# Attention on one core: reciprocals of the softmax sums taken on 16 columns after a trip through DMA, and weighting steps issued in four pairs a group

## The chip, the cores and the metric

The kernel runs on one core of a Trainium2 chip. The metric is the time of one execution on the device in microseconds, given as the median of several runs. The profile is of one further execution, with its own time. TensorE is called PE here, VectorE DVE, ScalarE ACT, GpSimd POOL, and SyncE, which issues most of the transfers, SP.

## The reference

Four gated residual blocks follow each other on x (2 batches, 512 tokens, width 1024): a quantised product with the context, a feed-forward layer with eight low-rank adapters, a cross-attention on the context, and a mixture of 2 experts out of 3. The change lies in the third block. Cut to it:

```python
q = (query @ Wq).reshape(b, sq, 32, 32).transpose(0, 2, 1, 3)   # 32 heads of 32
k = (key @ Wk).reshape(b, sk, 8, 32)...                         # 8 key/value heads
v = (value @ Wv).reshape(b, sk, 8, 32)...
k = jnp.repeat(k, 4, axis=1); v = jnp.repeat(v, 4, axis=1)
scores = jnp.einsum('bhqd,bhkd->bhqk', q, k) * 32 ** (-0.5)
probs = jax.nn.softmax(scores, axis=-1)                         # over 1024 keys
out = jnp.einsum('bhqk,bhkd->bhqd', probs, v)
x = x + jnp.tanh(g_xattn[1]) * (out @ Wo)
```

## The kernel before

The whole program is written out engine by engine, and semaphores alone order the engines. The attention is cut into 16 groups (2 batches by 8 key/value heads). A group has 4 query heads, 512 queries and 1024 keys, and 32 steps. In step `t` of group `g` PE issues, in this order:

- a *row score tile* (L866, `score_step`): queries on the partitions, 512 keys across, for a group further on (52 steps ahead). It goes to one of three PSUM banks (`s_bank`). DVE takes the maximum of each row from it (L1609, `maximum`), and frees the bank by that. The 32 pairs of maxima of a group are folded by one small reduction (L1616, `mxc`).
- a *turned score tile* (L948, in `group`): keys on the partitions, 512 queries across, with the row maximum subtracted by two extra rows of the operands. It goes to one of three other banks (`T_BANKS`). ACT takes the exponential from it (L1265) into `PB`, and frees the bank by that. Eight tiles of 128 keys by four heads make the 32 steps.
- in some steps, behind these, *weighting steps* (L879, `weigh`): the exponentials of 128 keys, four heads, times the values, in f32, 8 instructions each, into bank 5. Eight a group.
- in steps 2 and 18 one of the two `total` steps (L879 as well, with `onesf` as weights, 8 instructions): the sums of the exponentials of the group before, into bank 6, on all 32 partitions of a head alike.

In this text a *burst* is what PE issues of L879 in one go, and a *run* the steps between two bursts. Before the change a weighting step follows steps 2, 6, 10, ... 30, so that a group has six bursts with one L879 step and two bursts (at 2 and 18) with two, and runs of four steps.

Once a group, at `TURN_AT`, PE turns the folded maxima of the next group (L874), ACT copies them (L1240, `row_out`), DVE makes their remainder (L1624, `row_lows`, at `ROW_LO_AT`), and SP sends both rows into the query operand. The turned maxima take one of the three banks of the turned tiles, from `TURN_AT` until `row_lows` has read them; the turned tile of step `TURN_AT + 3` is the next to use that bank and waits for `row_lo`.

The rest of a group's work: POOL adds the exponentials in pairs of key tiles (L590, four a group) and sends the sums on by an accumulating transfer; ACT copies the weighted values out at step 3 (L1246), the sums at step 20 (L1256, into `p_total`) and the divided output at step 28 (L1250). DVE takes the reciprocals of the sums of the group before the last in four quarters of 128 columns (L1599, `invert`), at steps 2, 6, 10 and 14. POOL multiplies by them behind its second addition of a group (L572, `divide`), and makes the remainder behind its third (L577).

SP goes through each group in this order: the two maxima rows of the group (L428), then, once the last turned tile of the group before is done, the queries (L421) and keys (L415) of the group two ahead, three transfers each.

Groups 14 and 15 have few or no row score tiles left; in their place PE issues parts of the output projection (L911).

## Time and profile before

| | us |
|---|---|
| median of 3 runs | 1292.96 (1292.89 to 1294.55) |
| the profiled execution, its time | 1290.26 |
| its span, first to last instruction | 1288.4 |

Busy shares of the span: PE 97%, DVE 63%, POOL 53%, ACT 38%. The attention loop lies between 458 and 865 us. A PE instruction that waits for nothing starts about 0.22 us after the one before it; the duration that the profile gives for it (0.38 us) includes its way through the array, so successive ones overlap and the starts are what counts. The same holds for DVE and ACT in a smaller measure: the start of the next says how long an instruction holds its engine.

### The profile page before, as it was taken

The page shows a single profiled execution, that of the slowest core. Times are in us where ns is not written, and L with a number is a line of the kernel's source. Part 1 is how long each engine was busy: PE and PEld are TensorE (multiplying, and loading weights), DVE is VectorE, ACT ScalarE, POOL GpSimd, SP SyncE. Part 2 cuts the span into 40 slices and gives each one's busy share as a digit, 9 for nine tenths or more (in the row PEclk, how much of TensorE's full clock was granted, in tenths as well). Part 3 has the DMA queues.
Part 4 walks back from the last instruction along what each step waited for, and adds up shares of the span by engine and source line. Part 5 has one row for each costly group of instructions (what it writes and reads, how often), then busy time and mean ns, then how long its engine had stood idle before and what let it go on. Part 6 is the DMA issues. An engine that isn't in the chain of part 4 may idle for free.

```text
span 1288.4 us, 17618 instructions
## 1 busy us (share of the span) xinstructions
PE 1243.5 (97%) x6696; PEld 532.5 (41%) x6696; DVE 814.6 (63%) x1433; ACT 487.7 (38%) x853; POOL 680.7 (53%) x300
## 2 busy tenths in 40 slices
PE   7879989999999989999999999999999999999998
PEld 4545544444444422222222222234554444444444
DVE  6677762233345678989998999625555855737632
ACT  3459431011110157777777777762163010010000
POOL 6000997720004268889889888991073553534510
PEclk8989999999999999999999999999999999999999
DMA  8347133200024224545444544431063342533301
GB/s 327 115 137 255 33 115 115 83 16 0 1 64 131 90 66 110 111 90 119 109 106 97 115 109 101 90 75 33 17 214 114 98 148 88 176 112 98 114 6 60
DMA packets 44524, 130.69 MB, mean 101 GB/s; under 512 B 6817, under 2 KB 17057, under 8 KB 40353
## 3 DMA queue, kind: packets, MB, share of 16 engines
q1 hardware_dynamic: 37536, 91.94, 22.1%
q0 software_dynamic: 4608, 33.56, 12.9%
q10 hardware_dynamic: 2304, 4.20, 0.9%
q8 instruction: 47, 0.77, 0.2%
q14 instruction: 29, 0.23, 0.1%
HBM read 85.49 MB, written 10.49 MB: 74 GB/s over the span
## 4 chain that ended last, share of the span: by engine, by line
PE 76%; DVE 16%; ACT 3%; issue 3%; DMA 1%; SPq 1%; POOL 1%; ACTq 0%; POOLq 0%; DVEq 0%
PE bank L624 45%; PE bank L879 9%; DVE mxp L1609 7%; PE bank L911 7%; PE bank L866 6%; PE bank L948 5%; DVE xn L1599 2%; PE bank L699 1%; DVE R L1349 1%; PE bank L711 1%; ACT XTh L1088 1%; DVE stats L1362 1%; DMA b1t<-b_in 1%; DVE XTl L1496 1%; ACT R L1086 1%
## 5 line engine op out<-in xcount | busy, mean ns | idle before, releaser
L1609 DVE TENSOR_REDUCE mxp<-bank 128x1 f32<-128x512 f32 x512 | 320.3, 680 | 59.2 <-PE bank L866 58.9
L1265 ACT ACTIVATE R<-bank 128x512 f32<-128x512 f32 x512 | 273.8, 601 | 114.6 <-PE bank L948 111.6
L624 PE MATMUL bank<-XTh,R 128*128 128x512 bf16 x896 | 277.7, 379 | 0.0
L590 POOL TENSOR_TENSOR R<-R 128x2048 f32<-128x2048 f32 x48 | 218.7, 4558 | 35.5 <-ACT R L1265 29.5
L624 PE MATMUL bank<-R 128*128 128x512 bf16 x960 | 209.2, 379 | 0.0
L624 PE MATMUL bank<-XTl,R 128*128 128x512 bf16 x448 | 169.9, 379 | 0.0
L612 POOL TENSOR_TENSOR R<-stage_pair,R 128x1024 bf16<-128x1024 f32 x32 | 75.0, 2359 | 144.8 <-DVE R L1758 86.5
L624 PEld LDWEIGHTS bank<-R 128*128 128x128 bf16 (+1 forms) x960 | 93.9, 98 | 113.3
L866 PE MATMUL bank<-R 96*128 96x512 bf16 x352 | 134.6, 382 | 4.8 <-DVE mxp L1609 3.0
L879 PE MATMUL bank<-R,stage_c 128*32 128x512 f32 x1024 | 136.4, 604 | 0.5 <-ACT R L1265 0.5
L948 PE MATMUL bank<-R 98*128 98x512 bf16 x352 | 133.9, 380 | 1.9 <-ACT R L1265 1.9
L624 PEld LDWEIGHTS bank<-XTh,R 128*128 128x128 bf16 x896 | 87.8, 98 | 105.1 <-issue 0.6
L500 POOL TENSOR_TENSOR R<-stage_pair,zero 128x1024 f32 (+1 forms) x35 | 67.4, 1926 | 88.8 <-DMA stage_pair<-wts_in 75.7
L612 POOL TENSOR_TENSOR R<-stage_c,R 128x1024 bf16<-128x1024 f32 x32 | 73.6, 2312 | 53.6 <-DVE R L1758 50.2
L1323 ACT ACTIVATE R<-bank,b1t 128x512 f32<-128x512 f32 x32 | 21.9, 687 | 206.4 <-PE bank L624 206.4
L1496 DVE TENSOR_TENSOR XTl<-bank,XTh 128x512 bf16<-128x512 f32 (+1 forms) x48 | 30.7, 681 | 82.2 <-ACT XTh L1181 80.0
L866 PEld LDWEIGHTS bank<-R 96*128 96x128 bf16 x352 | 34.1, 97 | 112.8 <-DVE mxp L1609 85.5
L502 POOL TENSOR_TENSOR R<-stage_pair,R 128x1024 f32 (+1 forms) x35 | 75.4, 2153 | 5.3 <-POOL R L500 4.7
L1599 DVE RECIPROCAL xn<-p_total 128x128 f32<-128x128 f32 x64 | 59.2, 937 | 27.7 <-POOL xn L572 27.7
L590 POOL TENSOR_TENSOR stage_pair<-R 128x2048 f32<-128x2048 f32 x16 | 73.9, 4616 | 2.3 <-ACT R L1265 1.2
L532 POOL TENSOR_TENSOR X<-X,R 128x1024 f32<-128x1024 f32 x8 | 18.6, 2349 | 101.7 <-DVE R L1489 101.7
L649 PE MATMUL bank<-R 128*128 128x512 bf16 x192 | 51.5, 424 | 20.4 <-DVE R L1349 13.7
(194 smaller groups left out, 1598.5 us busy)
## 6 DMA issues: line engine op xcount, KB each, us to landing
stage_pair<-wts_in SPq DMA_DIRECT2D x35, 512.0 KB, 3.6
R<-R POOLq DMA_DIRECT2D x16, 1024.0 KB, 7.0
stage_pair<-R POOLq DMA_DIRECT2D x16, 1024.0 KB, 7.0
stage_pair<-w_in SPq DMA_DIRECT2D x32, 512.0 KB, 3.5
stage_c<-w_in SPq DMA_DIRECT2D x32, 512.0 KB, 3.6
R<-q_scr SPq DMA_DIRECT2D x48, 128.0 KB, 2.4
XTh<-ctx_nat_in SPq DMA_DIRECT2D x11, 512.0 KB, 4.0
XTh<-ctx_t_in SPq DMA_DIRECT2D x9, 512.0 KB, 5.1
```

The source lines that it names most:

```text
L500: pool.tensor_tensor(hi, stage_w[stage][:, :], zero[:, :].to_broadcast([P, D]), ALU.add).then_inc(wt_hi, 1)
L502: pool.tensor_tensor(lo, stage_w[stage][:, :], hi, ALU.subtract).then_inc(wt_done, 1)
L590: pool.tensor_tensor(PS[(0, 1, 2, 1)[j]], PB[2 * j % 4], PB[2 * j % 4 + 1], ALU.add).then_inc(p_add, 1)
L612: pool.tensor_tensor(lo[:, cols], stage_e[(n - N_WT) % RING_E][:, :], hi[:, cols], ALU.subtract).then_inc(wt_done, 1)
L624: mm = pe.matmul(o, a, m, start=first and a is ah and bs is bh, stop=last and a is al)
L866: pe.matmul(bank[s_bank(u)][:, :], QS[g % 3][0:96, h * S + qt * P:h * S + (qt + 1) * P], KS[g % 3][0:96, kh * HALF:(kh + 1) * HALF], start ...
L879: mm = pe.matmul(out_bank[h * HD:(h + 1) * HD, :], weights, probs[:, h * S:(h + 1) * S], start=first, stop=last)
L911: mm = pe.matmul(outs[h], a[i][:, cols], b[i][:, k * D + h * HALF:k * D + (h + 1) * HALF], start=k == 0 and i == 0, stop=k == KT - 1 and i ...
L948: pe.matmul(bank[t_bank(g, t)][:, :], KS[g % 3][0:98, kt * P:(kt + 1) * P], QS[g % 3][0:98, h * S:(h + 1) * S], start=True, stop=True).the ...
L1265: act.activation(PB[kt % 4][:, h * S:(h + 1) * S], bank[t_bank(g, t)][:, :], ACT.Exp, scale=float(HD) ** -0.5).then_inc(exp_done, 1)
L1599: dve.reciprocal(rec[:, cols], p_sum[:, cols]).then_inc(rec_done, 1)
L1609: dve.tensor_reduce(mxp[head // REP % 2][:, m, n // 2, n % 2:n % 2 + 1], bank[s_bank(u)][:, :], AX.X, ALU.max).then_inc(s_max, 1)
```

## The change

Two things are done. First, the sums of a group are no longer inverted on all their columns. Since the 32 partitions of a head hold the same sums, SP sends one row of 512 of each head into a tile `few` of 32 partitions by 16 columns a head (four transfers, `sums_in`); DVE inverts 128 by 16 values in one instruction (`invert_few`, after step 8); SP writes them to a DRAM scratch, waits for that, and reads them back, one row of 512 spread over the 32 partitions of each head (four transfers, `reciprocals_in`). The last two groups keep the old way. Second, the weighting steps are issued two by two, after steps 2, 10, 18 and 26. `TURN_AT` and `ROW_LO_AT` each move up by one step.

```diff
@@ -68,11 +68,14 @@
 Q_KEYS = 3
 LEAD = 20
 ROWS = REP * TB
-TURN_AT = 16
-ROW_LO_AT = 18
+TURN_AT = 17
+ROW_LO_AT = 19
 T_BANKS = (2, 3, 4)
 TOTAL_AT = (2, 18)
 SUM_OUT_AT = 20
+FEW_AT = 8
+FEW = REP * S // P
+FEW_GROUPS = GROUPS - 2
 O_HI_AT = 28
@@ -146,6 +149,7 @@
         mv = [sb(f"mv{i}", [P, 2], F32) for i in range(2)]
         lnv = [sb(f"lnv{i}", [P, 7], F32) for i in range(2)]
         p_total = sb("p_total", [P, S], F32)
+        few = sb("few", [P, 2 * FEW], F32)
         carrier = sb("carrier", [P, 1], F32)
         rterm = sb("rterm", [P, TT], F32)
         rowq = sb("rowq", [P, TT], F32)
@@ -216,6 +220,7 @@
         k_scr = nc.dram_tensor("k_scr", [B, 2, KVD, SC], BF16, kind="Internal").ap()
+        r_scr = nc.dram_tensor("r_scr", [REP, S], F32, kind="Internal").ap()
         q_scr = nc.dram_tensor("q_scr", [KT, B, 2, P, S], BF16, kind="Internal").ap()
@@ -295,6 +300,10 @@
         o_out = sem("o_out")
         sum_out = sem("sum_out")
         rec_done = sem("rec_done")
+        few_in = sem("few_in")
+        few_rec = sem("few_rec")
+        few_out = sem("few_out")
+        rec_in = sem("rec_in")
         o_mul = sem("o_mul")
         o_hi = sem("o_hi")
         o_lo = sem("o_lo")
@@ -428,6 +437,24 @@
                     sp.dma_start(QS[g % 3][row:row + 1, :].rearrange("o (r n) -> o r n", r=ROWS),
                                  src[:, :]).then_inc(row_in, 16)
+            def sums_in(g):
+
+                sp.wait_ge(sum_out, g + 1)
+                for h in range(REP):
+                    sp.dma_start(few[h * HD:(h + 1) * HD, 0:FEW],
+                                 p_sum[h * HD:h * HD + 1, :].rearrange("o (i n) -> o i n", n=FEW)).then_inc(few_in, 16)
+
+            def reciprocals_in(g):
+
+                sp.wait_ge(few_rec, g + 1)
+                if g > 0:
+                    sp.wait_ge(rec_in, 16 * REP * g)
+                    sp.wait_ge(o_mul, g)
+                sp.dma_start(r_scr.rearrange("h (i n) -> (h i) n", n=FEW), few[:, FEW:2 * FEW]).then_inc(few_out, 16)
+                sp.wait_ge(few_out, 16 * (g + 1))
+                for h in range(REP):
+                    sp.dma_start(rec[h * HD:(h + 1) * HD, :], r_scr[h:h + 1, :].to_broadcast([HD, S])).then_inc(rec_in, 16)
+
             sp.wait_ge(k_out, 16 * 2 * B)
             sp.wait_ge(nat_mm, 2 * TT)
             for g in range(Q_KEYS):
@@ -446,10 +473,14 @@
                 sp.wait_ge(q_out[slot], 16 * 2 * B * KT // 4)
             for g in range(1, GROUPS):
                 rows_in(g)
+                if g >= 2:
+                    sums_in(g - 2)
                 if g + 2 < GROUPS:
                     sp.wait_ge(st_mm, STEPS * g)
                     queries_in(g + 2)
                     keys_in(g + 2)
+                if g >= 2:
+                    reciprocals_in(g - 2)
             reg = sp.alloc_register("expert_sp")
@@ -568,7 +599,10 @@
                 if g > 0:
                     pool.wait_ge(o_lo, g)
-                pool.wait_ge(rec_done, 4 * (g + 1))
+                if g < FEW_GROUPS:
+                    pool.wait_ge(rec_in, 16 * REP * (g + 1))
+                else:
+                    pool.wait_ge(rec_done, 4 * (g - FEW_GROUPS + 1))
                 pool.tensor_tensor(onat, o_raw[g % 2], rec, ALU.mult).then_inc(o_mul, 1)
             def divided_lo(g):
@@ -949,11 +983,9 @@
                               QS[g % 3][0:98, h * S:(h + 1) * S], start=True, stop=True).then_inc(st_mm, 1)
                     if g + 1 < GROUPS and t == TURN_AT:
                         max_rows(g + 1)
-                    if t % 4 == 2:
-                        if t > 4:
-                            weigh(g, t // 4 - 1)
-                        elif g > 0:
-                            weigh(g - 1, KT - 1)
+                    if t % 8 == 2 and (g > 0 or t > 8):
+                        for kt in (t // 4 - 2, t // 4 - 1):
+                            weigh(g - (kt < 0), kt % KT)
                     if g > 0 and t in TOTAL_AT:
                         total(g - 1, TOTAL_AT.index(t))
                     if STEPS * g + t >= STEPS * GROUPS - 6 * KT:
@@ -989,6 +1021,7 @@
                 pe.matmul(bank[7][:, b * 2 * TB:(b + 1) * 2 * TB], onesf[:, :],
                           AM[:, b, :, :].rearrange("p a t -> p (a t)"), start=True, stop=True).then_inc(as_mm, 1)
+            weigh(GROUPS - 1, KT - 2)
             weigh(GROUPS - 1, KT - 1)
             output_tile(1)
             total(GROUPS - 1, 0)
@@ -1251,8 +1284,10 @@
             def sums_out(g):
                 act.wait_ge(one_mm, 2 * (g + 1))
-                if g > 0:
-                    act.wait_ge(rec_done, 4 * g)
+                if g > FEW_GROUPS:
+                    act.wait_ge(rec_done, 4 * (g - FEW_GROUPS))
+                elif g > 0:
+                    act.wait_ge(few_in, 16 * REP * g)
                 act.activation(p_sum, bank[6][:, :], ACT.Copy).then_inc(sum_out, 1)
             def exp_group(g):
@@ -1594,10 +1629,15 @@
                 cols = slice(quarter * S // 4, (quarter + 1) * S // 4)
                 if quarter == 0:
                     dve.wait_ge(sum_out, g + 1)
-                    if g > 0:
-                        dve.wait_ge(o_mul, g)
+                    dve.wait_ge(o_mul, g)
                 dve.reciprocal(rec[:, cols], p_sum[:, cols]).then_inc(rec_done, 1)
+
+            def invert_few(g):
+                dve.wait_ge(few_in, 16 * REP * (g + 1))
+                if g > 0:
+                    dve.wait_ge(few_out, 16 * g)
+                dve.reciprocal(few[:, FEW:2 * FEW], few[:, 0:FEW]).then_inc(few_rec, 1)
             def maximum(u):
@@ -1643,8 +1683,8 @@
                         maximum(u)
                     if g + 1 < GROUPS and t == ROW_LO_AT:
                         row_lows(g + 1)
-                    if g > 1 and t < STEPS // 2 and t % 4 == 2:
-                        invert(g - 2, t // 4)
+                    if g > 1 and t == FEW_AT:
+                        invert_few(g - 2)
             for quarter in range(4):
                 invert(GROUPS - 2, quarter)
```

What stands in the program now is shown at three places. On PE, in the middle of a group, around steps 16 to 20 (L866 and L948 are the two score tiles, L874 the turning of the maxima, bank 5 the weighting, bank 6 the sums), before the change:

```order
L874 MATMUL bank4<-identf,mxc 16x128 [waits exp_done,mx_done]
L866 MATMUL bank0<-stage_c1,R1 128x512 [waits s_max]
L948 MATMUL bank2<-R1 128x512 [waits exp_done]
L866 MATMUL bank1<-stage_c1,R1 128x512 [waits s_max]
L948 MATMUL bank3<-R1 128x512 [waits exp_done]
L879 MATMUL bank5<-R5,stage_c1 32x512 [waits exp_done]
L879 MATMUL bank5<-R5,stage_c1 32x512 x3
L879 MATMUL bank6<-stage_pair,onesf 32x512 [waits ps_sum1]
L879 MATMUL bank6<-stage_pair,onesf 32x512 x3
L866 MATMUL bank7<-stage_c1,R1 128x512 [waits s_max]
L948 MATMUL bank4<-R1 128x512 [waits row_lo]
```

and with it (L900 and L982 are the score tiles now, L913 the L879 of before):

```order
L900 MATMUL bank1<-stage_c1,R1 128x512 [waits s_max]
L982 MATMUL bank3<-R1 128x512 [waits exp_done]
L913 MATMUL bank5<-R5,stage_c1 32x512 [waits exp_done]
L913 MATMUL bank5<-R5,stage_c1 32x512 x3
L913 MATMUL bank5<-R5,stage_c1 32x512 [waits exp_done]
L913 MATMUL bank5<-R5,stage_c1 32x512 x3
L913 MATMUL bank6<-stage_pair,onesf 32x512 [waits ps_sum1]
L913 MATMUL bank6<-stage_pair,onesf 32x512 x3
L900 MATMUL bank7<-stage_c1,R1 128x512 [waits s_max]
L982 MATMUL bank4<-R1 128x512 [waits exp_done]
L900 MATMUL bank0<-stage_c1,R1 128x512 [waits s_max]
L982 MATMUL bank2<-R1 128x512 [waits row_lo]
```

The burst after step 18 has three L913 steps in place of two, and the turned tile that waits for `row_lo` is the second one behind the burst, where it was the first.

On DVE, from the fold of the maxima (at step 11) to the `row_l` remainder, before:

```order
L1616 TENSOR_REDUCE mxc<-mxp1 128x16 [waits nm_turned,s_max]
L1609 TENSOR_REDUCE mxp0<-bank1 128x1 [waits mx_done,s_mm]
L1609 TENSOR_REDUCE mxp0<-bank7 128x1 [waits s_mm]
L1609 TENSOR_REDUCE mxp0<-bank0 128x1 [waits s_mm]
L1599 RECIPROCAL xn1<-p_total 128x128
L1609 TENSOR_REDUCE mxp0<-bank1 128x1 [waits s_mm]
L1609 TENSOR_REDUCE mxp0<-bank7 128x1 [waits s_mm]
L1609 TENSOR_REDUCE mxp0<-bank0 128x1 [waits s_mm]
L1609 TENSOR_REDUCE mxp0<-bank1 128x1 [waits s_mm]
L1624 TENSOR_TENSOR row_l<-bank4,row_h 16x128 [waits row_in,row_hi]
L1609 TENSOR_REDUCE mxp0<-bank7 128x1 [waits s_mm]
```

and with the change:

```order
L1656 TENSOR_REDUCE mxc<-mxp1 128x16 [waits nm_turned,s_max]
L1649 TENSOR_REDUCE mxp0<-bank1 128x1 [waits mx_done,s_mm]
L1649 TENSOR_REDUCE mxp0<-bank7 128x1 [waits s_mm]
L1649 TENSOR_REDUCE mxp0<-bank0 128x1 [waits s_mm]
L1649 TENSOR_REDUCE mxp0<-bank1 128x1 [waits s_mm]
L1649 TENSOR_REDUCE mxp0<-bank7 128x1 [waits s_mm]
L1649 TENSOR_REDUCE mxp0<-bank0 128x1 [waits s_mm]
L1649 TENSOR_REDUCE mxp0<-bank1 128x1 [waits s_mm]
L1649 TENSOR_REDUCE mxp0<-bank7 128x1 [waits s_mm]
L1664 TENSOR_TENSOR row_l<-bank2,row_h 16x128 [waits row_in,row_hi]
L1649 TENSOR_REDUCE mxp0<-bank0 128x1 [waits s_mm]
```

Of the group's four reciprocals (one of them is seen here) none is left, and `row_l` stands one maximum later.

On SP, one group, before:

```order
L428 DMA R1<-row_h 1x16x128 [waits row_lo]
L428 DMA R1<-row_l 1x16x128
L421 DMA R1<-q_scr 32x4x512 [waits st_mm]
L421 DMA R1<-q_scr 32x4x512 x2
L415 DMA R1<-k_scr 32x1024 x3
```

and with the change:

```order
L437 DMA R1<-row_h 1x16x128 [waits row_lo]
L437 DMA R1<-row_l 1x16x128
L444 DMA few<-p_total 32x1x16 [waits sum_out]
L444 DMA few<-p_total 32x1x16 x3
L430 DMA R1<-q_scr 32x4x512 [waits st_mm]
L430 DMA R1<-q_scr 32x4x512 x2
L424 DMA stage_c1<-k_scr 32x1024 x3
L453 DMA r_scr<-few 128x16 [waits o_mul,rec_in,few_rec]
L456 DMA xn1<-r_scr 32x512 [waits few_out]
L456 DMA xn1<-r_scr 32x512 x3
```

The four sums go in front of the queries, and the write and the four reads of the reciprocals behind the keys, in front of the next group's rows.

## Rows read from the trace of the kernel before

**Rows 1.** The page: busy time, share and instructions of each engine

```profile
PE 1243.5 (97%) x6696; PEld 532.5 (41%) x6696; DVE 814.6 (63%) x1433; ACT 487.7 (38%) x853; POOL 680.7 (53%) x300
```

**Rows 2.** Windows: groups 1, 8, 14, then 2-13: us; PE, PEld, DVE, ACT, POOL busy

```profile
484.22:508.99 24.77, 24.77 (x150) 7.41 (x153) 20.25 (x35) 17.61 (x36) 20.28 (x8) 1.00 0.51 110
662.69:688.31 25.62, 25.22 (x150) 7.25 (x153) 23.24 (x39) 18.39 (x37) 22.35 (x10) 1.00 0.49 107
816.43:840.94 24.51, 24.08 (x145) 6.84 (x148) 13.65 (x21) 18.16 (x37) 22.41 (x10) 1.00 0.43 87
508.99:816.43 307.44, 302.70 (x1744) 87.00 (x1748) 278.83 (x457) 220.65 (x433) 271.37 (x109) 1.00 0.49 106
```

**Rows 3.** The chain that ended last, at the loop's end: start us, us

```profile
864.83 1.06 PE bank L879 x8
```

**Rows 4.** Timeline, PE, around a double and a single burst: start us, us

```profile
662.33 0.38 PE L948 MATMUL bank<-R,stage_c 98*128 98x512 bf16 x1
...
664.50 0.39 PE L866 MATMUL bank<-R 96*128 96x512 bf16 x1
...
666.03 0.38 PE L948 MATMUL bank<-R,stage_c 98*128 98x512 bf16 x1
...
666.37 1.06 PE L879 MATMUL bank<-R,stage_c 128*32 128x512 f32 x8
...
667.37 0.39 PE L866 MATMUL bank<-R 96*128 96x512 bf16 x1
```

**Rows 5.** Timeline, opening of group 0, seven steps with no burst between

```profile
458.40 0.39 PE L866 MATMUL bank<-R 96*128 96x512 bf16 x1 [1.41 <-DVE R L1637]
...
458.82 4.28 DVE L1609 TENSOR_REDUCE mxp<-bank 128x1 f32<-128x512 f32 x7 [0.48 <-PE bank L866]
...
459.72 0.38 PE L866 MATMUL bank<-R 96*128 96x512 bf16 x1
...
460.17 0.39 PE L866 MATMUL bank<-R 96*128 96x512 bf16 x1
...
461.37 0.39 PE L866 MATMUL bank<-R 96*128 96x512 bf16 x1
```

**Rows 6.** Timeline of group 8, DVE: fold of maxima, remainder of the rows

```profile
671.38 0.63 DVE L1609 TENSOR_REDUCE mxp<-bank 128x1 f32<-128x512 f32 x1
...
672.14 1.88 DVE L1609 TENSOR_REDUCE mxp<-bank 128x1 f32<-128x512 f32 x3
...
677.13 0.27 DVE L1624 TENSOR_TENSOR row_l<-bank,row_h 16x128 bf16<-16x128 f32 x1
```

**Rows 7.** Timeline of group 8, step 3: its tile, the copy behind the exponential

```profile
664.72 0.38 PE L948 MATMUL bank<-R,stage_c 98*128 98x512 bf16 x1
...
665.14 0.60 ACT L1265 ACTIVATE R<-bank 128x512 f32<-128x512 f32 x1 [1.64 <-PE bank L948]
...
665.63 0.59 ACT L1246 ACTIVATE stage_c<-bank 128x512 f32<-128x512 f32 x1
...
666.11 1.58 ACT L1265 ACTIVATE R<-bank 128x512 f32<-128x512 f32 x3
```

**Rows 8.** Timeline of group 8, POOL, second addition to the division

```profile
675.37 4.52 POOL L590 TENSOR_TENSOR R<-R 128x2048 f32<-128x2048 f32 x1 [1.81 <-ACT R L1265]
...
680.80 1.57 POOL L572 TENSOR_TENSOR xn<-stage_c,xn 128x512 f32<-128x512 f32 x1
```

**Rows 9.** Groups by line and form, reciprocals: xcount, busy us, mean ns

```profile
L1599 DVE RECIPROCAL xn<-p_total 128x128 f32<-128x128 f32 x64 | 59.2, 937 | 27.7 <-POOL xn L572 27.7
...
L1738 DVE RECIPROCAL rv<-rv 128x8 f32<-128x8 f32 x1 | 0.2, 203 | 0.0
```

**Rows 10.** DMA of groups 2 to 13: issues, KB each, us to landing

```profile
R<-q_scr SPq DMA_DIRECT2D x36, 128.0 KB, 2.4
...
R<-row_l SPq DMA_DIRECT2D x13, 4.0 KB, 1.8
```

**Rows 11.** Timeline, SP, one group's queries: three issues

```profile
661.43 1.27 SPq L421 DMA_DIRECT2D R<-q_scr  x3
```

## The prediction

> **What bounds the kernel now.** I read the page's busy shares first [rows 1]: PE 97%, nothing else above 63%. That says PE, but not why. So I went to the attention loop, where the whole change lies, and cut it into windows from the burst after step 2 of a group to that of the next [rows 2]; the reader is to see three kinds of group. Group 1, which has no reciprocals yet, takes 24.77 us with PE busy all of it. A middle group takes 25.62, the mean of groups 2 to 13 too (307.44 / 12), with PE busy 25.22, DVE 23.24, ACT 18.39, POOL 22.35. Group 14, whose row score tiles end at step 11, takes 24.51.
>
> Now what PE must do in a group. A score tile costs 0.22 us: six from 458.40 to 459.72 [rows 5]. A burst costs, from the last tile before it to the first behind it and less one tile, 667.37 - 666.03 - 0.22 = 1.12 us with one L879 step and 664.50 - 662.33 - 0.22 = 1.95 with two [rows 4]. A group has 64 tiles (14.0), six single bursts (6.7), two double ones (3.9) and the turning (0.1): 24.7 us. That is group 1. So PE is the bound, and the reciprocals cost a middle group 25.62 - 24.77 = 0.85 us by making DVE late in freeing the three banks of the row score tiles.
>
> **The two gains.** The reciprocals leave DVE: 4 x 0.94 us a group [rows 9] and in their place one on 16 columns. No such row is there; between 203 ns on 8 columns and 937 on 128 it is (937 - 203) / 120 = 6.1 ns a column, so some 0.25 us (0.20 to 0.94 by the two rows themselves). It stands behind the sixth maximum of a run of eight, which no tile of the run waits for, as seen below, so it costs nothing; without that cover it would be its 0.25 us, 3 us in all. Gain: at most the 0.85.
>
> The bursts: four pairs of single steps merge. Two singles cost 2.24, a double 1.95, so 0.29 a pair, 1.2 a group. A burst of three is not in the trace; I take 1.95 + (1.95 - 1.12) = 2.78; at most it is 1.95 + 1.12 = 3.07, a burst that shares nothing, and then a group is 0.6 us dearer. PE's own work falls to 24.7 - 1.2 = 23.5.
>
> **What the merging costs: runs of eight steps.** DVE holds each row tile 0.60 us ((4.28 - 0.68) / 6, seven maxima) [rows 5], PE issues one each 0.44. In a run of four that is harmless: three banks take the lead and the burst lets DVE catch up. The trace has one place with a longer run, the opening of group 0, seven steps with no burst [rows 5]: row tiles start 1.32 (fourth), 1.77 (fifth) and 2.97 us (seventh) after the first. From the fifth on each waits for DVE, and the last two came 0.60 apart. As a rule with these numbers: a maximum starts 0.43 after its tile (458.40, 458.82) or 0.60 after the last one, lasts 0.68, and the tile three further on may start 0.06 after its end (the second maximum from 458.82 + 0.60 = 459.42 to 460.10; the fifth tile at 460.17). The eighth tile comes at 2.97 + 0.60 = 3.57 instead of 7 x 0.437 = 3.06: 0.5 us lost in a run of eight. DVE then idles through the burst, as nothing more can be put into three banks. Four runs a group: +2.0 us. It is lost in group 1 as well, where the reciprocals play no part, and it is more than both gains hold, 2.05 in all.
>
> Two things make it worse. The fold of the maxima stands behind step 11, now the first of a run: from one maximum to the next it is 672.14 - 671.38 = 0.76 with the fold between, instead of 0.60 [rows 6], and DVE sets the pace in that run: +0.16. And `row_l`, which stood in front of the maximum of step 19 and so ran inside the burst of step 18 (at 677.13) [rows 6], moves behind that maximum. Step 19's tile is issued behind the burst, so `row_l` now starts only 0.43 + 0.60 = 1.03 us behind the first tile of the new run, lasts 0.27, and the turned tile of step 20 comes at 1.36 instead of 0.67. Behind it ACT is late: an exponential starts 0.42 behind its tile, holds ACT 0.49 and lasts 0.60, and a copy holds it 0.48 [rows 7]. So step 20's starts at 1.36 + 0.42 = 1.78, the copy of the sums at 2.27, the exponentials of steps 21, 22 and 23 at 2.75, 3.24 and 3.73, and the last ends at 4.33. The turned tile of step 26 uses its bank: 4.39, against 3.57 + 0.22 = 3.79 in a run that DVE alone slows. +0.6. By DVE's side alone it would be about 0.4, and it can't be nothing, for the tile of step 19 can't come before the burst. The turning (0.1) hides, as PE waits there.
>
> So a middle group: 14.0 + 2 x 1.95 + 2 x 2.78 = 23.5, + 2.0 + 0.16 + 0.6 = 26.2 us, against 25.62: +0.6.
>
> **The transfers.** SP gets nine more a group. Issues cost it 1.27 / 3 = 0.42 us each [rows 11]; they land 1.8 to 2.4 us later [rows 10]. The sums leave behind step 20 and are wanted at step 8 of the next group, over 10 us later. The maxima rows go ahead of them and the queries wait for the end of the group anyway, so what is queued behind them isn't late. The reciprocals: DVE's stands behind three steps, a burst of three and six maxima (1.3 + 2.8 + 0.43 + 5 x 0.60 + 0.68), so at about 8.3 us into a group, write 0.42 + 2.4, four reads 4 x 0.42 + 2.4, so at about 15.2. POOL wants them behind its second addition, which starts at the end of the exponential of step 15 (three steps, 2.8, a run of 4.0, a double burst 1.95 and five steps of the next run up to that end, 3.2: about 13.3), and takes 680.80 - 675.37 = 5.4 us up to the division [rows 8]: 18.7. They are 3.5 us early and cost nothing. Beyond that POOL has 25.62 - 22.35 = 3.3 us idle in a middle group [rows 2]. SP is free again before the next maxima rows at step 20. The Trainium skill (DMA: Bandwidth & Descriptors, on the two cost components) gives each transfer about 2.0 us fixed whatever its size, mostly the receipt, longest when HBM is the target, as in the write here; by it the chain would be ready some 0.8 us earlier, and the rows agree, with 1.8 us for 4 KB.
>
> **Sum.** Groups 2 to 13: 12 x 0.6 = +7.2. Group 1: 26.2 - 24.77 = +1.45. Group 0 has the long runs too but half its steps stand under POOL's late start: half of that, +0.7. Group 14 loses DVE's load at step 11, but ACT then sets the pace in the runs with a copy: the eighth turned tile waits for the fifth exponential, 0.64 + 0.49 + 4 x 0.48 + 0.60 + 0.06 = 3.7 against 3.3; with its first two runs still DVE's, +0.9. Group 15: three such runs take about what the merging gives, 0. Behind the last step stands a double burst in place of a single one, on the chain at 864.83 [rows 3]: +0.8. In all +11.0. The profiled execution took 1290.26 and would take 1301.3; the median of the runs lies 2.7 above it, so I forecast 1292.96 + 11.0 = **1304 us**.
>
> **The rivals.**
> (a) *The long runs are absorbed*, PE is the bound at 23.5 us: the bursts go to banks 5 and 6, so DVE and ACT can empty the others meanwhile. For it: DVE's sum falls from 23.24 to about 19.7. Against it: the opening [rows 5], where three banks were not enough for seven steps. Time: 12 x (25.62 - 23.5) + 2 x 1.2 for groups 1 and 14 = -28, 1265 us. 5%. With half of the stalls gone, 23.5 + 1.4 = 24.9, it is 12 x -0.7: 1284. Another 4%. This is the side of faster; it decides if an eight-step run loses under 0.3 us. The Trainium skill (Perfetto Trace Analysis, on matmuls under Optimizing Tensor Performance) wants independent matmul groups to rotate through different PSUM banks so that their evacuation overlaps the next group's matmuls, which speaks for (a); the trace shows the overlap ending at three banks [rows 5].
> (b) *Only `row_l` and the fold are covered*, the period is 25.5 to 25.7. Then groups 2 to 13 are even and the rest adds 3.3: 1296. For it: ACT's part of that sum is my own chain over five instructions. 16%, reaching from 1294 to 1300.
> (c) *The reciprocals come late*. From DVE's instruction to the last read I count 7 us. Up to 10 nothing waits, up to 13 only POOL's idle time goes, and each further us costs 14 us in all (15 us: 1304 + 28 = 1332). The small pieces of 64 bytes speak for it, the 3.5 us of slack against it. 7%.
> (d) *No change*, gains and losses even: within 0.2% (2.6 us, what a measurement of this kernel can tell). 5%.
> My own case holds 63%, 1300 to 1308.
>
> The range takes in (b) from 1297 and my own case to 1309: 1297 to 1309. Faster by over 0.2%: 0.09. Within: 0.07, (d) and the edge of (b). Slower: 0.84.
>
> **What would show it.** In the profile after: period 26.2 between bursts; row tiles at 0.60 from the fifth of a run on, each run 0.5 longer; PE waiting for the row maxima more than before though DVE is less busy (about 20 us a group); a turned tile at step 20 waiting 0.7 us for `row_l`; bursts of 16 and 24 L879 in turn; the division on POOL starting as before behind its addition, not behind a transfer. The forecast is wrong if the eighth row tile of a run comes before 3.3 us, or if POOL is found waiting for the reciprocals.

## The result, and the profile after

The median after is 1310.09 us (1308.52 to 1313.51, 4 runs) against 1292.93 before (4 runs): ratio 1.0138, 95% interval 1.0116 to 1.0161, so +17.2 us. The sign was forecast, the size was not: +11.0 stood in the prediction, and the time lies 1.1 us above the upper end of its range. The profiled execution took 1309.13 us, with a span of 1307.0.

The page of after, busy time of each engine (as [rows 1]):

```profile
PE 1248.8 (96%) x6696; PEld 536.3 (41%) x6696; DVE 772.1 (59%) x1391; ACT 483.9 (37%) x853; POOL 680.7 (52%) x300
```

DVE has lost 42.5 us of work, and the kernel is slower all the same. The windows of after answer to [rows 2], in the same order: groups 1, 8, 14, then 2 to 13 together, with the length of the window, the busy time of PE, PEld, DVE, ACT and POOL, the granted clock, the DMA share and GB/s.

```profile
487.92:514.32 26.40, 25.54 (x150) 7.45 (x153) 19.97 (x35) 17.71 (x36) 20.02 (x8) 1.00 0.48 104
673.11:699.51 26.40, 25.42 (x150) 7.63 (x153) 20.07 (x36) 18.09 (x38) 22.25 (x10) 1.00 0.52 112
831.48:856.95 25.47, 24.22 (x145) 7.34 (x148) 7.27 (x14) 17.40 (x37) 21.37 (x9) 1.00 0.46 94
514.32:831.48 317.16, 304.98 (x1745) 91.43 (x1748) 240.85 (x421) 216.70 (x433) 271.50 (x109) 1.00 0.52 113
```

A middle group takes 26.40 us now (25.62 before; 26.2 was forecast), group 1 as much (24.77 before), group 14 25.47 (24.51 before). DVE's work in group 8 fell from 23.24 to 20.07 us, and PE has 0.98 us idle in it, where it had 0.40.

PE's part of the timeline of after, from step 3 to step 26 of group 8, shows where the time lies. L900 is a row score tile, L982 a turned tile, L913 a burst:

```profile
675.76 0.39 PE L900 MATMUL bank<-R 96*128 96x512 bf16 x1
...
679.33 0.39 PE L900 MATMUL bank<-R 96*128 96x512 bf16 x1
679.55 0.38 PE L982 MATMUL bank<-R,stage_c 98*128 98x512 bf16 x1
...
681.72 0.39 PE L900 MATMUL bank<-R 96*128 96x512 bf16 x1
...
685.51 0.39 PE L900 MATMUL bank<-R 96*128 96x512 bf16 x1
685.74 0.38 PE L982 MATMUL bank<-R,stage_c 98*128 98x512 bf16 x1
686.05 1.92 PE L913 MATMUL bank<-R,stage_c 128*32 128x512 f32 x16
687.79 1.04 PE L913 MATMUL bank<-stage_pair,onesf 128*32 128x512 f32 x8
688.76 0.39 PE L900 MATMUL bank<-R 96*128 96x512 bf16 x1
...
690.12 0.39 PE L982 MATMUL bank<-R,stage_c 98*128 98x512 bf16 x1 [0.53 <-DVE row_l L1664]
...
693.16 0.39 PE L982 MATMUL bank<-R,stage_c 98*128 98x512 bf16 x1
```

Each run can be read here against the prediction. In the first, the eighth row tile starts 679.33 - 675.76 = 3.57 us after the first, as forecast. (On the way there ACT has a part as well, with its copy at step 3: the sixth starts 2.50 us after the first, where DVE alone would allow 2.37.) In the second, which has the fold of the maxima in it, 685.51 - 681.72 = 3.79 (3.57 + 0.16 = 3.73 forecast). In the third, the turned tile of step 20 starts 690.12 - 688.76 = 1.36 behind the first tile (1.36 forecast) after waiting for `row_l`, and that of step 26 4.40 behind it (4.39 forecast). The burst of three takes 688.76 - 685.74 - 0.22 = 2.80 (2.78), that of two 681.72 - 679.55 - 0.22 = 1.95 (1.95).

DVE's `row_l` there, behind the maximum of step 19 (from 689.19) now, where [rows 6] had it inside the burst:

```profile
689.80 0.27 DVE L1664 TENSOR_TENSOR row_l<-bank,row_h 16x128 bf16<-16x128 f32 x1
```

The waits of after between 508 and 860 us (who waits for whom, us in all, times, longest):

```profile
PEld bank L900 <- DVE mxp L1649: 74.3, 189, 0.8
...
PE bank L982 <- DMA R<-row_l: 0.6, 1, 0.6
```

The first line is no measure of the loss. PE's weight loads wait 74.3 us for the maxima here, and the same line of before has 115.3, though the runs lose more now. Most of before's can't have cost anything, since PE had only 307.44 - 302.70 = 4.7 us idle in groups 2 to 13 [rows 2]: a weight load also waits while the matmuls ahead of it still run. The starts of the tiles are what counts. The second line is one tile of group 4 that waited for the row of maxima.

Two of the DMA issues of after between 508 and 840 us (xcount, KB each, median us to landing; [rows 10] had 1.8 for `row_l`):

```profile
few<-p_total SPq DMA_DIRECT2D x50, 2.0 KB, 4.7
...
R<-row_l SPq DMA_DIRECT2D x12, 4.0 KB, 6.5
```

And the trip of one group's reciprocals, first SP, then POOL, from the timeline:

```profile
653.66 0.34 SPq L453 DMA_DIRECT2D r_scr<-few  x1
659.16 1.70 SPq L456 DMA_DIRECT2D xn<-r_scr  x4
```

```profile
651.17 0.87 POOL L627 DMA_DIRECT2D stage_pair<-R  x1 [0.30 <-POOL R L624]
...
658.90 4.54 POOL L624 TENSOR_TENSOR R<-R 128x2048 f32<-128x2048 f32 x1 [0.89 <-DMA stage_pair<-R]
...
664.36 1.56 POOL L606 TENSOR_TENSOR xn<-stage_c,xn 128x512 f32<-128x512 f32 x1
```

The write of 8 KB was out for 659.16 - 653.66 = 5.5 us, where 2.8 was counted. The last read, issued by 660.86, lands some 2.0 us later, about 662.9. The division starts at 664.36, still behind its addition and not behind a transfer: 3.5 us of slack were forecast, 1.5 are left.

### The profile page after: what moved, and what is told of

It reads as the page before. It is cut to its first block, busy times and chain, and to the rows that moved or that the text cites. A ratio compares the mean times of both kernels' runs of the same rounds, so it can differ in the third digit from the quotient of the medians.

```text
span 1307.0 us, 17715 instructions
## 1 busy us (share of the span) xinstructions
PE 1248.8 (96%) x6696; PEld 536.3 (41%) x6696; DVE 772.1 (59%) x1391; ACT 483.9 (37%) x853; POOL 680.7 (52%) x300
## 4 chain that ended last, share of the span: by engine, by line
PE 78%; DVE 8%; ACT 6%; issue 4%; DMA 1%; POOL 1%; SPq 0%; ACTq 0%; POOLq 0%; DVEq 0%
PE bank L658 44%; PE bank L913 11%; PE bank L900 7%; PE bank L982 7%; PE bank L945 6%; ACT R L1300 2%; PE bank L733 1%; DVE R L1384 1%; DVE mxp L1649 1%; PE bank L745 1%; ACT XTh L1121 1%; POOL R L624 1%; DVE stats L1397 1%; ACT stage_c L1279 1%; ACT p_total L1291 1%
## 5 line engine op out<-in xcount | busy, mean ns | idle before, releaser
L1300 ACT ACTIVATE R<-bank 128x512 f32<-128x512 f32 x512 | 269.7, 621 | 133.9 <-PE bank L982 130.8
L624 POOL TENSOR_TENSOR R<-R 128x2048 f32<-128x2048 f32 x48 | 218.4, 4550 | 37.8 <-ACT R L1300 29.8
L982 PE MATMUL bank<-R 98*128 98x512 bf16 x352 | 134.8, 383 | 11.4 <-DVE row_l L1664 5.3
L900 PE MATMUL bank<-R 96*128 96x512 bf16 x352 | 135.1, 384 | 2.3 <-DVE R L1677 1.4
L913 PE MATMUL bank<-R,stage_c 128*32 128x512 f32 x1024 | 124.5, 603 | 0.2 <-ACT R L1300 0.2
L624 POOL TENSOR_TENSOR stage_pair<-R 128x2048 f32<-128x2048 f32 x16 | 73.5, 4592 | 15.2 <-ACT R L1300 15.2
L900 PEld LDWEIGHTS bank<-R 96*128 96x128 bf16 x352 | 34.0, 97 | 92.4 <-DVE mxp L1649 57.4
L945 PE MATMUL bank<-R,XTh 128*128 128x512 bf16 x256 | 71.0, 385 | 0.0
```

Of the source, the lines that this page charges most:

```text
L624: pool.tensor_tensor(PS[(0, 1, 2, 1)[j]], PB[2 * j % 4], PB[2 * j % 4 + 1], ALU.add).then_inc(p_add, 1)
L900: pe.matmul(bank[s_bank(u)][:, :], QS[g % 3][0:96, h * S + qt * P:h * S + (qt + 1) * P], KS[g % 3][0:96, kh * HALF:(kh + 1) * HALF], start ...
L913: mm = pe.matmul(out_bank[h * HD:(h + 1) * HD, :], weights, probs[:, h * S:(h + 1) * S], start=first, stop=last)
L945: mm = pe.matmul(outs[h], a[i][:, cols], b[i][:, k * D + h * HALF:k * D + (h + 1) * HALF], start=k == 0 and i == 0, stop=k == KT - 1 and i ...
L982: pe.matmul(bank[t_bank(g, t)][:, :], KS[g % 3][0:98, kt * P:(kt + 1) * P], QS[g % 3][0:98, h * S:(h + 1) * S], start=True, stop=True).the ...
L1300: act.activation(PB[kt % 4][:, h * S:(h + 1) * S], bank[t_bank(g, t)][:, :], ACT.Exp, scale=float(HD) ** -0.5).then_inc(exp_done, 1)
```

## Where the 17 us lie

The loop of after, cut from the start of one group's first turned tile to the next, gives this. To keep the scatter of single executions small I take two profiles of each kernel, with those of e4 and e5 below (mean spans 1306.5 and 1288.9, a difference of 17.6):

| | forecast | found |
|---|---|---|
| ahead of the loop | 0 | +0.8 |
| group 0 | +0.7 | +1.6 |
| group 1 | +1.45 | +1.6 |
| groups 2 to 13 | +7.2 | +10.0 |
| group 14 | +0.9 | +1.0 |
| group 15 | 0 | 0.0 |
| behind the last step | +0.8 | +2.7 |
| in all | +11.0 | +17.6 |

Only the rows of groups 1 to 15 are steady from one execution to another. The loop's start and group 0 scatter by one or two microseconds in one and the same program, as e4 and e5 show.

## The experiments

**e1 and e2, each part alone.** e1 has the reciprocals on 16 columns and keeps the eight bursts, `TURN_AT` 16 and `ROW_LO_AT` 18 of before. e2 has nothing but the bursts:

```diff
-                    if t % 4 == 2:
-                        if t > 4:
-                            weigh(g, t // 4 - 1)
-                        elif g > 0:
-                            weigh(g - 1, KT - 1)
+                    if t % 8 == 2 and (g > 0 or t > 8):
+                        for kt in (t // 4 - 2, t // 4 - 1):
+                            weigh(g - (kt < 0), kt % KT)
...
+            weigh(GROUPS - 1, KT - 2)
```

> The reciprocals go by transfers on 16 columns, but bursts, turning and row_l stand as before. Theory of the banks (the loss comes from runs of eight steps): PE is the bound in every group as in group 1 of before, period 24.77 us instead of 25.62 in groups 2 to 13, about 24.3 in group 14: 12 x 0.85 + 0.2 = 10 us faster than before, about 1282.5. Theory of the transfers (the nine transfers a group delay something): it keeps part of the loss of the change, over 1293. Theory of the clock (PE pays at half clock behind idle times outside the loop's rhythm): it keeps only the part of the loss that lies outside groups 1 to 15, about 4 us, so 1287.

> The weighting steps go two by two, the four reciprocals a group stay on DVE as before (row_l and the turning too, at 16 and 18). Theory of the banks: the reciprocals stand inside the runs in which DVE sets the pace, so each counts in full and is no longer hidden in a burst; stepping through the starts with the durations of before gives 27.4 us for groups 2 to 13, 25.7 for group 1, 26.3 for group 14: about +24 us, 1317, slower than the whole change. Theory of the transfers: bursts alone gain 1.2 us a group, under 1293.

Measured: e1 1288.87 us against 1292.54, ratio 0.9963 [0.9948, 0.9977]; one of its ten executions took 5081.54 us, for which I have no cause, and it is not in the ratio. e2 1320.41, ratio 1.0221 [1.0197, 1.0245]. Windows of groups 2 to 13, e1, then e2:

```profile
510.23:811.97 301.74, 298.55 (x1742) 87.98 (x1741) 244.06 (x421) 218.69 (x433) 269.00 (x107) 1.00 0.55 119
```

```profile
511.45:840.37 328.92, 306.88 (x1742) 91.87 (x1740) 278.53 (x458) 216.88 (x433) 271.57 (x108) 1.00 0.46 99
```

e2 has 328.92 / 12 = 27.41 us a group, as expected: the pairs of weighting steps by themselves cost 1.8 us a group, because two of the four reciprocals, behind steps 6 and 14, now stand inside a run in which DVE sets the pace. From its first row tile to its eighth such a run takes 4.37 and 4.59 us in e2, where after has 3.57 and 3.79: 0.80 more each. e1 has 25.14 on the mean, where 24.77 was expected, and its groups differ: eight take 24.8 to 25.1, four 25.2 to 26.2. So the reciprocals' way through DMA gives back 0.48 us a group of the 0.85 that it could. That was a miss in time as well (1288.9 against the 1282.5 expected), and e7 and e8 follow it up.

**e3, `row_l` back inside the burst.** The kernel after, with one number changed:

```diff
-ROW_LO_AT = 19
+ROW_LO_AT = 18
```

> The changed kernel with row_l in front of the maximum of step 19 again (one number). Theory of the banks: row_l runs inside the burst of step 18 and costs nothing, the run behind it is 0.6 us shorter: period 25.7 to 25.8 us instead of 26.4, about 9 us faster than the changed kernel, 1301. If row_l's place is not what the run waits for: no change, 1310.

Measured: 1300.8 us, ratio 1.0062 [1.0039, 1.0085]. Its window of groups 2 to 13, and `row_l` on DVE from the timeline, inside the burst that starts at 580.85:

```profile
514.80:824.35 309.55, 305.79 (x1742) 92.83 (x1740) 239.91 (x422) 215.59 (x433) 271.54 (x108) 1.00 0.54 116
```

```profile
580.85 1.92 PE L913 MATMUL bank<-R,stage_c 128*32 128x512 f32 x16
...
581.97 0.27 DVE L1664 TENSOR_TENSOR row_l<-bank,row_h 16x128 bf16<-16x128 f32 x1
```

A group takes 25.77 in all but the first of them, 0.63 less than after: this is the term of `row_l` (+0.6), measured. The later `row_l` alone costs 12 x 0.63 = 7.6 us in the middle groups and 0.6 in group 1, nearly half of the 17. (e3 is 10.1 us faster than e4, the kernel after run beside it, but e4 has 1.7 us at a low clock behind the loop, and e3 hasn't.)

**e4 and e5, both kernels once more.** The kernel after and the kernel before, unchanged, for the scatter between executions and for a second profile of each.

> The changed kernel once more, beside the others on this chip. Period 26.4 in the loop. Its profile had 1.3 us more than before ahead of the loop and 1.7 us more behind it, at half the granted clock. If these belong to the change they are there again; if they belong to single executions they are elsewhere or gone, and the time falls towards 1307.

> The kernel before, for a second profile. All profiles since have group 0 at 26.4 to 29.0 us where the first profile of before had 24.3, and PE at half the granted clock there behind an idle time of 2.0 us or more. If that belongs to single executions, this profile can show it too (group 0 over 26 us, a single burst of 1.9 us instead of 1.06), and the change is not to be charged with it. If it belongs to the change, group 0 is 24.3 again. Periods 24.77, then 25.62.

Measured: 1310.89 us, ratio 1.0142 [1.0119, 1.0164], and 1294.11 us, ratio 1.0002 [0.9988, 1.0016]. Groups 1 to 15 agree within 0.03 us with the first profile in each. What differs is the start of the loop (457.7 to 459.9) and group 0: 24.34 and 26.17 us before, 26.41 and 27.21 after. What goes with it is seen in PE's timeline. In before, at step 18 of group 0:

```profile
472.45 0.39 PE L948 MATMUL bank<-R 98*128 98x512 bf16 x1 [1.95 <-ACT R L1265]
472.77 1.06 PE L879 MATMUL bank<-R,stage_c 128*32 128x512 f32 x8
```

and in e5, the same program:

```profile
471.72 0.39 PE L948 MATMUL bank<-R 98*128 98x512 bf16 x1 [2.15 <-ACT R L1265]
472.04 1.78 PE L879 MATMUL bank<-R,stage_c 128*32 128x512 f32 x8
```

PE waited 1.95 us in the one and 2.15 in the other, and in the second its clock was then granted at about half. The windows view shows it: from that burst on, e5 had 0.53 of the full clock for 3.4 us (the figure ahead of the last two), which is near its lower level of 1.2 GHz. After had 0.61 at the same step behind a wait of 2.23 us, and its double burst took 3.06 us instead of 1.92.

```profile
472.04:475.43 3.39, 3.39 (x13) 0.73 (x13) 0.95 (x3) 1.32 (x3) 3.38 (x1) 0.53 0.01 2
```

The length of the wait doesn't decide it. In e8, whose bursts are those of before, the same tile comes behind the same 1.95 us, and already takes 0.61 us instead of 0.39; the clock is at 0.50 for the 6 us from there on:

```profile
474.02 0.61 PE L982 MATMUL bank<-R 98*128 98x512 bf16 x1 [1.95 <-ACT R L1301]
```

All fourteen profiles have a wait at this step, of 1.86 us (e9) to 3.50 (e6). Thirteen show the lower clock behind it, for 3 to 10 us; the first profile of before is the only one that doesn't. With the bursts of before group 0 took 25.8 to 29.1 us in the seven profiles with the stretch and 24.34 in the one without. So the 24.34 is the exception, and the stretch comes with and without the change.

Behind the loop the kernel after has a stretch of low clock at another place. In its chain that ended last the 48 L945 matmuls take 10.36 us each time but one:

```profile
944.65 11.98 PE bank L945 x48
```

and its window there:

```profile
943.65:947.30 3.65, 3.65 (x16) 1.82 (x15) 2.99 (x21) 1.08 (x2) 0.00 (x0) 0.60 0.02 4
```

In e4 the eight L733 matmuls at 942.76 took 1.80 us instead of 0.93. PE didn't wait for another engine ahead of this stretch: by the profile it went through 96 matmuls of three columns each. Both profiles of after have it, and neither of before; but e11 below, whose bursts are those of before, has it at the same place (48 matmuls in 12.05 us), and e2 and e3, with after's code behind the loop, don't. So it isn't the merged bursts that bring it; what does is open. The clock of e11 there:

```profile
919.50:922.60 3.10, 3.10 (x10) 1.12 (x8) 2.59 (x18) 1.09 (x2) 0.00 (x0) 0.54 0.00 0
```

Most of the rest of the 2.7 us behind the last turned tile is the double burst: the two `total` steps of the last group start 13.25 us behind that tile in after, e2, e3, e4 and e6, and 12.53 in the profiles with a single burst, so it costs 0.72.

**e6 and e10, is it the maxima?** e6 is the kernel after with the maximum taken over half of the columns, which leaves half of each row's keys out of it. e10 does this and leaves out the exponentials of half of the queries.

```diff
-    bank[s_bank(u)][:, :]
+    bank[s_bank(u)][:, 0:HALF // 2]
...
-    PB[kt % 4][:, h * S:(h + 1) * S], bank[t_bank(g, t)][:, :]
+    PB[kt % 4][:, h * S:h * S + S // 2], bank[t_bank(g, t)][:, 0:S // 2]
```

> The changed kernel, with the row maxima taken over 256 of the 512 columns of each tile; the other half of each maximum is left out. DVE then holds a tile about 0.33 us instead of 0.60. Theory of the banks: DVE no longer sets the pace in runs of eight, ACT does (0.49 a tile and its copies), and row_l still costs: period 25.7 to 25.8 us instead of 26.4, about 8 us faster than the changed kernel. If long runs cost PE something of its own (weights, the bursts themselves), the period stays at 26.4.

> The changed kernel with maxima and exponentials both over 256 of 512 columns; the other halves are left out. Neither DVE nor ACT can set the pace in a run of eight any more. PE's own work is 23.5 us a group by the sum of the prediction. If that sum and the price of a burst of three (2.8 us) are right and nothing else bounds, the period is 23.5. If the circle of POOL's additions and its accumulating transfer is the next bound, 24.5 us as counted in e1, the period is 24.5 to 25, and the rival that the long runs are absorbed could never have given more than that.

Measured: e6 1301.02 us, ratio 1.0048 [1.0029, 1.0067]. e10 ran once, 1300.9 us. e6's maxima by line and form, and its window of groups 2 to 13:

```profile
L1649 DVE TENSOR_REDUCE mxp<-bank 128x1 f32<-128x256 f32 x512 | 215.6, 423 | 208.3 <-PE bank L900 203.6
```

```profile
511.27:821.87 310.60, 298.57 (x1742) 90.12 (x1742) 165.50 (x422) 214.36 (x433) 270.81 (x108) 1.00 0.54 116
```

With a maximum of 423 ns in place of 682 most groups take 25.81, not 26.40: so DVE does set the pace in the runs of after, but right beneath it lies ACT's. In the run from step 3 the eighth row tile still comes 3.48 us after the first, and the last three are 0.49 apart, which is what an exponential holds ACT [rows 7]. In e10, with both halved, it comes after 673.72 - 670.65 = 3.07, as in a run that nobody slows:

```profile
670.65 0.39 PE L900 MATMUL bank<-R 96*128 96x512 bf16 x1
...
673.72 0.38 PE L900 MATMUL bank<-R 96*128 96x512 bf16 x1
```

So the loss within a plain run is that of the two engines that empty the banks, and of nothing else. Yet the groups of e10 take 25.5 to 26.6 us (26.0 on the mean), and neither 23.5 nor the 24.5 to 25 that its expectation had. The time lies now in other places, at the bursts and at single turned tiles, on a PE that is idle a good deal. The waits name a third limit:

```profile
POOL R L624 <- DMA stage_pair<-R: 31.9, 13, 3.2
...
ACT R L1300 <- POOL R L624: 20.9, 21, 2.2
```

ACT waits for a free `PB` buffer, POOL for the landing of its accumulating transfer. Why a group takes 26.0 us there, and not the 24.5 that I had counted for POOL's circle of additions and transfer, is not shown. Rival (a), 23.5 us a group, was out of reach by two more limits than the one I had argued from.

**e7 and e8, what the transfers cost.** e7 is e1 without the nine transfers a group: DVE inverts 16 columns of `p_total` where they lie, and POOL multiplies by what `rec` holds, so that the sums don't divide the output. e8 is e1 with the whole trip earlier (`FEW_AT` 2 instead of 8) and the division ahead of POOL's second addition instead of behind it.

```diff
-                if g >= 2:
-                    sums_in(g - 2)
...
-                if g >= 2:
-                    reciprocals_in(g - 2)
...
-                dve.reciprocal(few[:, FEW:2 * FEW], few[:, 0:FEW]).then_inc(few_rec, 1)
+                dve.reciprocal(few[:, FEW:2 * FEW], p_sum[:, 0:FEW]).then_inc(few_rec, 1)
```

> e1 with the nine transfers a group left out: the reciprocals of 16 columns are still taken, but never spread, and POOL divides by what lies in the tile. Theory of contention: e1 fell short (1288.9 instead of 1282.5) since the small transfers stretch POOL's accumulating transfers, 7.0 us alone and 7.5 in the middle with them, up to 9; without them they land in 7.0 again, POOL and PE no longer wait for them, and the time is about 1283. Theory of the ring: the circle of POOL's additions and its transfer is by itself 24.5 us long and stalls at a period of 24.77 anyway: 1288 again.

> e1 with the small reciprocal behind step 2 instead of 8 and POOL's division in front of its second addition instead of behind it, so that it lies in the time in which POOL waits for its transfer. The circle addition, transfer, addition gets 1.6 us shorter, 22.9 instead of 24.5: period 24.77 in all groups from 1 to 13, and 1283 us. If the reciprocals aren't back by then (the write took 5.5 to 6.4 us to land, not 2.4), POOL waits for them and it is no faster than e1, 1289.

Measured: e7 1285.41 us against 1293.6, ratio 0.9926 [0.9906, 0.9946]; e8 1288.86, ratio 0.9957 [0.9938, 0.9975], no better than e1, where 1283 was expected. e7's window of groups 2 to 13:

```profile
513.66:810.86 297.20, 297.20 (x1741) 88.96 (x1740) 244.24 (x421) 218.03 (x433) 268.94 (x107) 1.00 0.51 109
```

297.20 / 12 = 24.77 in every group, PE busy all of it. So what e1 lost, 0.37 us a group, goes with the transfers. Not all of it need be theirs: e9 and e12 below have no small transfers either, and single groups of 26.04 and 25.76 us all the same, 0.13 to 0.15 a group on the mean. The transfers don't cost by being late. POOL's division never waited for the reciprocals in e1, and in e8, which asks for them earlier, once, for 1.6 us. POOL's timeline of e1 shows what happens, in a long group (637.24 to 663.53) and a good one (663.53 to 688.00). L624 are the additions, L627 the issues of the accumulating transfers:

```profile
637.24 4.59 POOL L624 TENSOR_TENSOR R<-R 128x2048 f32<-128x2048 f32 x1
642.13 0.88 POOL L627 DMA_DIRECT2D stage_pair<-R  x1 [0.30 <-POOL R L624]
...
651.00 4.54 POOL L624 TENSOR_TENSOR R<-R 128x2048 f32<-128x2048 f32 x1 [3.10 <-DMA stage_pair<-R]
...
663.53 4.57 POOL L624 TENSOR_TENSOR R<-R 128x2048 f32<-128x2048 f32 x1
668.39 0.88 POOL L627 DMA_DIRECT2D stage_pair<-R  x1 [0.30 <-POOL R L624]
...
675.55 4.53 POOL L624 TENSOR_TENSOR R<-R 128x2048 f32<-128x2048 f32 x1 [1.38 <-DMA stage_pair<-R]
...
688.00 4.67 POOL L624 TENSOR_TENSOR R<-R 128x2048 f32<-128x2048 f32 x1
```

POOL's next but one addition can't start before the transfer has landed. When that takes 675.55 - 668.39 = 7.2 us, POOL comes round in 24.47 us, just below the 24.77 of PE. When it takes 651.00 - 642.13 = 8.9, in 26.29, and two others wait. PE itself does, whose `total` step needs the landed sums, as its timeline has it at the same moment:

```profile
650.91 1.07 PE L913 MATMUL bank<-stage_pair,onesf 128*32 128x512 f32 x8 [0.91 <-DMA stage_pair<-R]
```

And ACT waits for a free `PB` buffer, 5.4 us in 11 times between 508 and 860 us. The landing of these 1 MB transfers, min, median and max, was 6.9, 7.5 and 9.1 us in e1 and 6.9, 7.0 and 8.8 in e7. Before had 6.9, 7.0 and 9.2 and 0.85 us more a group to hide it. So landings of about 9 us come without the small transfers too; with them the median is longer.

**e9, e11 and e12, without transfers.** If the reciprocals must leave the runs and the transfers cost too, there is a third way: the kernel before, its bursts as they were, with the same 512 columns inverted in seven pieces, one behind each maximum that precedes a burst, where DVE is idle. In e9 (e12 is e9 again) the pieces stand at steps 26 and 30 of the group before and 2 to 18; in e11 they start one burst earlier, at step 22, and the division goes ahead of POOL's second addition.

```diff
+PIECES = {22: (0, 64), 26: (64, 128), 30: (128, 192), 2: (192, 320), 6: (320, 384), 10: (384, 448), 14: (448, 512)}
...
+                    if g >= 2 and j == 1:
+                        divide(g - 2)
...
+                dve.reciprocal(rec[:, cols], p_sum[:, cols]).then_inc(rec_done, 1)
...
-                    if g > 1 and t < STEPS // 2 and t % 4 == 2:
-                        invert(g - 2, t // 4)
+                    behind = g - (1 if t in (22, 26, 30) else 2)
+                    if t in PIECES and 0 <= behind < SPREAD:
+                        invert_piece(behind, t)
```

> The kernel before with its reciprocals cut to the idle time of DVE, no transfer and no change of the bursts: seven pieces (64 columns behind steps 26 and 30 of the group before, 128 behind step 2, 64 behind steps 6, 10, 14 and 18) in place of four of 128 behind steps 2, 6, 10 and 14. A piece of 64 columns holds DVE about 0.46 us by the two rows of before, and a period of four steps and a single burst is 2.87 us against 4 x 0.60 + 0.46 = 2.86 of DVE. Theory of the banks: DVE just keeps up, the period is 24.77 in groups 2 to 13 and there are no small transfers to stretch POOL's: 10 us faster than before, 1283, as e7. If pieces cost more than their columns or stand in the way of the maxima, 25.0 to 25.6 and 1285 to 1293.

> e9 with all seven pieces one burst earlier (22, 26, 30 of the group before, 2, 6, 10, 14) and POOL's division in front of its second addition. In e9 the profile has three groups over 24.9 us (24.92, 26.04 and 24.86, 24.86), where POOL and PE waited for an accumulating transfer that took up to 9 us instead of 7. The division (1.57 us) now lies in that wait, so the circle is 1.6 us shorter. Theory of the ring: no group but the first is over 24.85, about 1.5 us faster than e9. If the stalls come by PE's own wait for the sums (step 18 and 2), nothing changes.

> e9 once more, on the same chip as e11: 8 us faster than before, 24.77 in most groups, and one or two groups (not always the same) at 25 to 26.

Measured: e9 1286.17 us, ratio 0.995 [0.9931, 0.9968]; e12 1286.86, ratio 0.9942 [0.992, 0.9963]; e11 **1283.66 us**, ratio 0.9929 [0.9903, 0.9956], ahead of both kernels. Window of groups 2 to 13 in e11, and POOL's waits for transfers in it, then in e12:

```profile
509.57:807.38 297.81, 297.46 (x1742) 89.06 (x1740) 278.94 (x493) 217.41 (x433) 270.48 (x108) 1.00 0.51 110
```

```profile
POOL R L598 <- DMA R<-R: 6.4, 12, 2.1
...
POOL R L598 <- DMA stage_pair<-R: 0.6, 1, 0.6
```

```profile
POOL R L596 <- DMA stage_pair<-R: 14.6, 9, 3.0
...
POOL R L596 <- DMA R<-R: 4.2, 3, 2.0
```

297.81 / 12 = 24.82 a group, 0.05 above PE's own 24.77. DVE does as much as before, 278.94 us against the 278.83 of [rows 2], and PE, idle for 0.35 us in all, loses next to nothing by it (POOL's division waits for the last piece, eight times, 0.4 us at most): only where DVE's work stands has changed. In e12 the middle groups take 24.92 on the mean and one of them 25.76; there the division stands between an addition and the next, and with it ahead of the second addition, in the time in which POOL waits for the landing anyway, the waits of 14.6 + 4.2 us become 0.6 + 6.4. One group of e11 (group 4) took 25.32, where none over 24.85 was expected. The intervals of e11 and e12 overlap, so that e11 is the better of the two is what their profiles say, not their times. It differs from e12 in two things, the pieces one burst earlier and the place of the division; no run takes them apart.

## Why the prediction was wrong in size

**What bounds the kernel, and the runs of eight.** Right, and to a few hundredths: 0.5 lost in a run by three banks that DVE holds 0.60 us each (3.57 forecast, 3.57 found; e6 shows that ACT alone would lose nearly as much there, 3.48), the fold (3.73 and 3.79), `row_l` (1.36 and 1.36, 4.39 and 4.40), the burst of three (2.78 and 2.80). e3 measured `row_l` by itself at 0.63 (0.6). The difference of e2 and e3 says that the reciprocals are worth 27.41 - 25.80 = 1.6 us a group once the runs are long, not 0.85; the sum didn't need this, since it started from PE's own work. A slip stands in that part: the runs of eight by themselves (2.0) are not "more than both gains hold, 2.05". It is the fold and `row_l` (0.16 + 0.6) that carried the loss above the gains; with `row_l` left where it was the middle groups are even within 0.2 (e3: 25.80 and 25.62). The kernel as a whole is not: e3 is still 8.3 us slower than before, so rival (d) would not have come then either.

**The step that failed is the Sum.** It failed in three of its terms.
The first is "Groups 2 to 13: 12 x 0.6 = +7.2", found +10.0. No mechanism is missing in a middle group; small errors, nearly all to one side, were taken times twelve. The bursts take 9.52 in place of 9.46 (2.81 each with three steps); each of the four runs loses 0.52, and 0.5 was taken; the fold costs 3.79 - 3.57 = 0.22, and not 0.16. The tiles (64 x 0.2185 = 13.98) and `row_l` (0.59 in that run) were right. With these, 13.98 + 9.52 + 2.08 + 0.22 + 0.59 = 26.39, and 26.40 is found. The difference of two numbers of 26 was the whole forecast, and 0.18 was a quarter of the 0.78 that was found. Another 0.7 us lies in groups 2 and 4 (26.68 and 26.85): in group 4 a turned tile waited for the row of maxima, and group 2 is 0.28 longer than its neighbours in e2, e3 and after alike, for which I have no cause.
The second is "Group 0 … half of that, +0.7", found +1.6. That figure can't be had from two profiles: 24.34 and 26.17 us stand in the same program of before, and the first is the one profile of fourteen without the stretch of low clock.
The third is behind the last step, "+0.8". The double burst did cost that (0.72), but a stretch at half clock added 1.7. It came in both profiles of after, but in e11 as well, with the bursts of before, and not in e2 and e3; what sets it off is open. A further 0.8 us lies ahead of the loop, where the change alters no instruction. The sum put these places at nothing without a reason, and own-case bounds of 4 us either side for a sum of six terms were too narrow for them.

**The transfers.** Right that POOL wouldn't wait for the reciprocals, so (c) did not come: the division stood behind its addition. But "write 0.42 + 2.4" was 5.5, and of the 3.5 us of slack 2.0 were used up. That they "cost nothing" was right for this kernel, and for the wrong reason. Alone (e1) they go with 0.37 us a group, through the landing of POOL's transfers; the long runs of after gave POOL 26.4 us for its round instead of 24.8, and hid that (its additions waited 3.3 + 1.1 us for landings between 508 and 860 us, 20.9 + 2.6 in e1). Two costs that hide each other don't add: parts alone, -0.48 (e1) and +1.79 (e2), give +1.3 a group, together they gave +0.8, in the kernel where `row_l` costs another 0.6.

**Rival (a)** was rightly put at little. It would have taken a DVE that holds a bank less long, an ACT that does (e6: 25.8), and a POOL that comes round faster (e10: 26.0). **Rival (b)** is nearly what e3 is, 25.80 us a group with `row_l` covered: 1300.8 us, where (b) said 1296. Its middle groups make 2.1 us of that difference, the rest lies outside them.

**What would show it.** Period, step 20, bursts and the division were as listed, and so were tiles at 0.60 in the run with the fold; in the run from step 3 they come 0.73, 0.49 and 0.58 apart, for ACT's copy. One was not: PE's recorded waits for the maxima were to grow, and fell from 115.3 to 74.3 us. Only the starts of the tiles show the loss.

## What to carry to other kernels

Where a producer fills a ring of N buffers and the consumer holds each longer than the producer needs for one, only a run not much longer than N is free, and every further step goes at the consumer's pace (with three banks, from the fifth tile on); merging the producer's other work into fewer, longer pieces lengthens the runs, and so can cost what it saves. Before work is moved off a busy engine, look for the stretches in which it idles anyway: the same reciprocals, cut into seven pieces and put there, gave 0.5 to 0.7% at no transfer at all, where one number, which put `row_l` one maximum later, had cost 0.6 us a group. And when a forecast is the small difference of two large sums, carry every hundredth, and take two profiles of before to see which places scatter by themselves.
